# A routed expert layer whose row movements go per slot of an expert instead of per tile of tokens

## The reference

```python
logits = xf @ Wg                                  # 2048 x 8
probs = jax.nn.softmax(logits, axis=-1)
top_vals, top_idx = jax.lax.top_k(probs, 2)
onehot = one_hot(top_idx.T.reshape(-1), 8)        # 4096 choices, first choices first
loc = (cumsum(onehot, axis=0) - 1) at the chosen expert
keep = loc < 640
gates = top_vals * keep, divided by their sum
...
hid = inp @ W_in[e]                               # inp: the kept rows of expert e, 640 x 256; W_in[e]: 256 x 1024
a, g = jnp.split(hid, 2, axis=-1)
out_e = (gelu(a) * g) @ W_out[e]                  # W_out[e]: 512 x 256
y = sum over the 2 choices of gate * row loc of out_e   # x = x + y; xf is the layer-normed x
```

## Time and profile before

| | us |
|---|---|
| median of three runs (3078.27 to 3094.05) | 3084.43 |
| the profiled execution, own time | 3079.66 |
| its span in the profile | 3078.0 |
| layer L1f in the span (1736.9 to 2087.0) | 350.1 |

### The profile page before, as it was taken

The page is one execution under the profiler, slowest core; times in us unless marked ns, Lnnn a source line. Parts: engine busy times, 40 slices in busy tenths (PEclk is TensorE's granted clock), DMA queues, the critical chain, the costliest instruction groups (busy, mean ns, idle before and its releaser), DMA issues. The chain is left out here.

```text
span 3078.0 us, 84125 instructions
## 1 busy us (share of the span) xinstructions
PE 2585.4 (84%) x36049; PEld 2147.0 (70%) x36049; DVE 1781.5 (58%) x3347; ACT 1359.2 (44%) x3398; POOL 607.1 (20%) x740
## 2 busy tenths in 40 slices
PE   6999788999949999999987719937987766999888
PEld 5888556677737888888875519935774645888657
DVE  5777675566664444444455416636775766666563
ACT  3777323455523444444321204406773243666442
POOL 3111002121022111111102040042320533222200
PEclk9999899999979999999986659978998688999999
DMA  2110012111031000000000223322221001111100
GB/s 74 35 34 16 16 28 62 57 57 30 17 96 42 16 16 16 16 16 2 2 22 2 71 106 105 120 75 85 89 72 32 2 2 48 44 48 43 44 1 28
DMA packets 118717, 129.78 MB, mean 42 GB/s; under 512 B 10606, under 2 KB 109882, under 8 KB 118362
## 3 DMA queue, kind: packets, MB, share of 16 engines
q1 hardware_dynamic: 113882, 110.93, 11.7%
q0 software_dynamic: 4480, 13.64, 1.3%
HBM read 105.67 MB, written 18.88 MB: 40 GB/s over the span
## 5 line engine op out<-in xcount | busy, mean ns | idle before, releaser
L940 ACT ACTIVATE s_ca_probs<-s_ca_scores,s_ca_neg_max 128x256 f32<-128x256 f32 x768 | 353.3, 483 | 12.0 <-DVE s_ca_neg_max L983 8.8
L983 DVE TENSOR_REDUCE s_ca_neg_max<-s_ca_scores 128x4 f32<-128x1024 f32 x192 | 234.2, 1221 | 102.6 <-PE s_ca_scores L851 54.6
L863 PE MATMUL s_ca_probs_flipped<-identity,s_ca_probs 128*128 128x128 f32 x1536 | 212.6, 282 | 15.9 <-ACT s_ca_probs L940 9.8
L1314 DVE RECIPROCAL s_cc_inv_sums<-s_cc_sums 128x512 f32<-128x512 f32 x32 | 107.5, 3358 | 182.5 <-PE s_cc_out L1214 182.5
L863 PEld LDWEIGHTS s_ca_probs_flipped<-identity,s_ca_probs 128*128 128x128 f32 x1536 | 167.5, 143 | 58.6 <-ACT s_ca_probs L940 26.3
L1928 DVE COPY s_mx_w_mixed<-s_mx_ps 128x512 f32<-128x512 f32 x256 | 163.8, 684 | 60.3 <-PE s_mx_ps L1775 45.1
L946 ACT COPY s_ca_probsT<-s_ca_probs_flipped 128x512 f32<-128x512 f32 x192 | 114.7, 597 | 173.0 <-PE s_ca_probs_flipped L863 173.0
L1883 ACT COPY s_mx_w_mixed<-s_mx_ps 128x512 f32<-128x512 f32 x256 | 137.3, 589 | 115.3 <-PE s_mx_ps L1762 95.2
L550 PE MATMUL s_ln_flip<-identity,s_ln_xn 128*128 128x128 f32 x352 | 64.9, 368 | 139.5 <-DVE s_ln_xn L532 139.2
L1134 POOL TENSOR_TENSOR s_cc_probs_of_both<-s_cc_probsT 128x1024 f32<-128x1024 f32 x32 | 76.8, 2400 | 521.1 <-DVE s_cc_probsT L1305 521.1
L777 POOL TENSOR_TENSOR s_ca_inv_spread<-s_ca_inv_sums,h_ca_own_half 128x128 f32<-128x128 f32 x192 | 72.6, 399 | 472.8 <-DVE s_ca_inv_sums L1004 472.8
(11 more groups left out here) (462 smaller groups left out, 7250.8 us busy)
## 6 DMA issues: line engine op xcount, KB each, us to landing
h_ca_ctxT<-in_ctxT SPq DMA_DIRECT2D x96, 256.0 KB, 3.0
h_mx_w_by_input<-in_L_ffn_eW1T SPq DMA_DIRECT2D x16, 512.0 KB, 5.2
h_mx_w_by_hidden<-in_L_ffn_eW2T SPq DMA_DIRECT2D x8, 1024.0 KB, 6.3
s_re_win<-in_L_ffn_W_in SPq DMA_DIRECT2D x8, 1024.0 KB, 7.1
h_ca_ctx<-in_ctx SPq DMA_DIRECT2D x32, 256.0 KB, 2.8
x_normed_transposed<-in_ctx SPq DMA_DIRECT2D x7, 1024.0 KB, 5.5
expert_queues<-s_rt_zeros SPq DMA_DIRECT2D x5, 1024.0 KB
s_re_rows<-expert_queues SPq DMA_DIRECT2D x8, 640.0 KB, 5.1
```

The lines of the kernel that those rows point to most:

```text
L863: last = nc.tensor.transpose(psT[:, 2 * a + c, :], PR[b % 2][:, 4 * n + a, c * P:(c + 1) * P], ident[:, :])
L940: last = nc.scalar.activation(PR[b % 2][:, p, :], psS[:, p // 2, (p % 2) * NKEY:(p % 2 + 1) * NKEY], ACT.Exp, bias=nmax[b % 2][:, p:p + 1] ...
L983: nc.vector.tensor_reduce(nmax[b % 2][:, 4 * n:4 * n + 4], psS[:, 2 * n:2 * n + 2, :].rearrange("p r (g k) -> p r g k", g=GR), AX_X, ALU.m ...
L1314: nc.vector.reciprocal(RD[:, :, :], psD[:, :, :]).then_inc(s_rd, 1)
```

## The change

The row movements go by slot of an expert (8 x 640 slots in 40 tiles of 128) instead of by tile of choices.

- The small weights, the constants and expert 0's weights are loaded in the normalisation stage, and TensorE computes the logits there, two pairs of tiles behind its transposes.
- The new router stage `route_tokens` keeps softmax, choices and counts. SP stores the normalised rows as they are (`xrows`, 2 MB), zeroes `results` (4 MB, one row for each choice and a spare row for each slot) and loads expert 1's weights. Expert 0's weights are split by ACT and GpSimd. DVE compares each choice's place with a counting row, so that a sum of 32 multiplications on TensorE gives for each slot the number of the choice that lies in it. From it come `TOKN` (which token's row to gather) and `SLOT` (which row of `results` to write). GpSimd gathers the rows of experts 0 and 1 with 10 indirect DMAs at the end of this stage.
- In `routed_experts` GpSimd gathers the five row tiles of expert e + 2 and scatters the five result tiles of expert e, with 5 indirect DMAs each. The loop is written out. No instruction of TensorE's `up`, `down` or `flip` changes.
- The final stage is gone: at the end of `routed_experts` SP waits for the scatters and loads the results with 16 contiguous DMAs of 256 KB in eight groups into `XN` and `XNT`; DVE adds and takes statistics per group of two tiles, with the same 32 + 16 instructions.

```diff
+class ExpertWeights:
...
+        self.XR = [sb("re_rows", [P, QT, DIM]) for _ in range(2)]
+        self.WI, self.WO = sb("re_win", [P, KC, 2 * F]), sb("re_wout", [P, F // P, DIM])
...
+        self.xrows = nc.dram_tensor("expert_inputs", (TOKENS, DIM), F32, kind="Internal").ap()
+        self.results = nc.dram_tensor("choice_results", (2 * TILES * P + self.E * self.CAP, DIM), F32, kind="Internal").ap()
...
+    def load(self, sp):
+        d = self.d
+        sp.dma_start(self.WG[:, :, :], rows_to_sbuf(d["L1_ffn_Wg"])).then_inc(self.s_wg, 16)
...
+        self.load_in(sp, 0)
+        self.load_out(sp, 0)
+    def gather(self, pool, e):
+        QT = self.CAP // P
+        for n in range(e * QT, (e + 1) * QT):
+            pool.indirect_dma_start(self.XR[e % 2][:, n - e * QT, :], None, self.xrows,
+                                    bass.IndirectOffsetOnAxis(self.TOKN[:, n:n + 1], 0)).then_inc(self.s_r[e % 2], 16)
+    def logits(self, pe, XNT, u):
+        if u == 0:
+            pe.wait_ge(self.s_wg, 16)
+        for t in (2 * u, 2 * u + 1):
+            for c in range(KC):
+                pe.matmul(self.psL[:, t * self.E:(t + 1) * self.E], XNT[:, c, t * P:(t + 1) * P], self.WG[:, c, :],
+                          start=(c == 0), stop=(c == KC - 1))
...
+                    if logits and u >= 2:
+                        pe.wait_ge(s_out, u - 1)
+                        logits(pe, XNT, u - 2)
+                if logits:
+                    for u in range(NU - 2, NU):
+                        pe.wait_ge(s_out, u + 1)
+                        logits(pe, XNT, u)
...
+def route_tokens(nc, XN, ones, held):
...
+            @block.sync
+            def _(sp):
+                for h in range(2):
+                    t = slice(h * TILES // 2, (h + 1) * TILES // 2)
+                    sp.dma_start(xrows.rearrange("(t p) n -> p t n", p=P)[:, t, :], XN[:, t, :]).then_inc(s_x, 16)
+                sp.wait_ge(s_z, 1)
+                for r in range(0, CHOICES * P, ZR):
+                    sp.dma_start(results[r:r + ZR].rearrange("(a p) n -> p a n", p=P), Z[:, :, :]).then_inc(s_q, 16)
+                sp.wait_ge(s_il, KC)
+                held.load_in(sp, 1)
+                sp.wait_ge(s_ol, 1)
+                held.load_out(sp, 1)
+                sp.wait_ge(s_q, 16 * (CHOICES * P // ZR))
+            @block.gpsimd
+            def _(pool):
+                nc.gpsimd.memset(Z[:, :, :], 0.0).then_inc(s_z, 1)
+                for c in range(KC):
+                    pool.wait_ge(s_ih, c + 1)
+                    nc.gpsimd.tensor_tensor(WIS[0][1][:, c, :], WI[:, c, :], WIS[0][0][:, c, :].bitcast(F32), ALU.subtract).then_inc(s_il, 1)
+                pool.wait_ge(s_oh, 1)
+                nc.gpsimd.tensor_tensor(WOS[0][1][:, :, :], WO[:, :, :], WOS[0][0][:, :, :].bitcast(F32), ALU.subtract).then_inc(s_ol, 1)
+                pool.wait_ge(s_eq, 1)
+                nc.gpsimd.tensor_tensor(B[:, :, 1, :], EQ[:, :, :], NUM[:, :].unsqueeze(2).broadcast_to([P, CHOICES, SLOTS]),
+                                        ALU.mult).then_inc(s_b, 1)
+                pool.wait_ge(s_x, 32)
+                pool.wait_ge(s_tok, 1)
+                held.gather(pool, 0)
+                held.gather(pool, 1)
+            @block.tensor
+            def _(pe):
+                pe.wait_ge(s_c0, 64)
+                nc.tensor.matmul(psN[:, 0:P], ones[:, :], BE[:, :], start=True, stop=True).then_inc(s_io, 1)
+                pe.wait_ge(s_ohc, 1)
+                flat = OH[:, :, :, :].rearrange("p k t e -> p (k t e)")
+                nc.tensor.matmul(psR[:, 0:CHOICES * E], BE[:, :], flat, start=True, stop=True)
+                nc.tensor.matmul(psT[:, 0:CHOICES * E], ones[:, :], flat, start=True, stop=True).then_inc(s_cn, 1)
+                pe.wait_ge(s_b, 2)
+                for n in range(CHOICES):
+                    pe.wait_ge(s_a, n // GROUP + 1)
+                    last = nc.tensor.matmul(psI[:, 0:2 * SLOTS], A[:, n, :], B[:, n, :, :].rearrange("p a h -> p (a h)"),
+                                            start=(n == 0), stop=(n == CHOICES - 1))
+                last.then_inc(s_in, 1)
...
+                act.wait_ge(s_io, 1)
+                nc.scalar.copy(IOTA[:, :], psN[:, 0:P]).then_inc(s_ct, 1)
+                act.wait_ge(s_mx, 1)
+                nc.scalar.activation(PRB[:, :, :], L[:, :, :], ACT.Exp).then_inc(s_e, 1)
+                for c in range(KC):
+                    act.wait_ge(held.s_wi, 16)
+                    nc.scalar.copy(WIS[0][0][:, c, :], WI[:, c, :]).then_inc(s_ih, 1)
+                act.wait_ge(held.s_wo, 16)
+                nc.scalar.copy(WOS[0][0][:, :, :], WO[:, :, :]).then_inc(s_oh, 1)
...
+                nc.vector.tensor_reduce(kept[:, :], KM[:, :, :], AX_X, ALU.add)
+                nc.vector.tensor_tensor(KB[:, :, :], KM[:, :, :], BASE[:, :].unsqueeze(1).broadcast_to(C), ALU.mult)
+                link(nc.vector.tensor_tensor(PLACE[:, :, :], PLACE[:, :, :], KM[:, :, :], ALU.mult))
+                nc.vector.tensor_scalar(far[:, :], kept[:, :], -1000.0, 1000.0, ALU.mult, ALU.add)
+                nc.vector.tensor_reduce(start[:, :], KB[:, :, :], AX_X, ALU.add)
+                link(nc.vector.tensor_reduce(loc[:, :], PLACE[:, :, :], AX_X, ALU.add))
+                nc.vector.scalar_tensor_tensor(far[:, :], start[:, :], 1.0 / P, far[:, :], ALU.mult, ALU.add)
+                link(nc.vector.tensor_scalar(q[:, :], loc[:, :], float(P), None, ALU.is_ge))
+                for j in range(2, QT):
+                    link(nc.vector.scalar_tensor_tensor(q[:, :], loc[:, :], float(j * P), q[:, :], ALU.is_ge, ALU.add))
+                nc.vector.scalar_tensor_tensor(lo[:, :], q[:, :], -float(P), loc[:, :], ALU.mult, ALU.add)
+                link(nc.vector.tensor_tensor(hi[:, :], q[:, :], far[:, :], ALU.add))
+                dve.wait_ge(s_ct, 1)
+                nc.vector.tensor_tensor(EQ[:, :, :], hi[:, :].unsqueeze(2).broadcast_to([P, CHOICES, SLOTS]),
+                                        IOTA[:, 0:SLOTS].unsqueeze(1).broadcast_to([P, CHOICES, SLOTS]), ALU.is_equal).then_inc(s_eq, 1)
+                dve.wait_ge(s_eq, 1)
+                nc.vector.tensor_scalar(B[:, :, 0, :], EQ[:, :, :], LANE[:, 0:1], None, ALU.mult).then_inc(s_b, 1)
+                for g in range(CHOICES // GROUP):
+                    n = slice(g * GROUP, (g + 1) * GROUP)
+                    nc.vector.tensor_tensor(A[:, n, :], lo[:, n].unsqueeze(2).broadcast_to([P, GROUP, P]),
+                                            IOTA[:, :].unsqueeze(1).broadcast_to([P, GROUP, P]), ALU.is_equal).then_inc(s_a, 1)
+                nc.vector.tensor_scalar(dump[:, :], IOTA[:, 0:SLOTS], float(P), LANE[:, 0:1], ALU.mult, ALU.add)
+                dve.wait_ge(s_in, 1)
+                link(nc.vector.tensor_copy(tile_of[:, :], psI[:, SLOTS:2 * SLOTS]))
+                link(nc.vector.scalar_tensor_tensor(number[:, :], tile_of[:, :], float(P), psI[:, 0:SLOTS], ALU.mult, ALU.add))
...
+                nc.vector.tensor_copy(TOKN[:, :], token[:, :]).then_inc(s_tok, 1)
...
+                nc.vector.tensor_copy(SLOT[:, :], number[:, :])
...
+def routed_experts(nc, X, ST, XNT, XN, ident, held):
...
+        YG = [XN[:, :, :], XNT[:, :, :].rearrange("p c n -> p (c n)").rearrange("p (t n) -> p t n", n=DIM)]
...
+            @block.sync
+            def _(sp):
+                for e in range(2, E):
+                    sp.wait_ge(s_il, e * KC)
+                    held.load_in(sp, e)
+                    sp.wait_ge(s_ol, e)
+                    held.load_out(sp, e)
+                for u in range(2):
+                    sp.wait_ge(s_st[u], 16 * QT * (E // 2))
+                for g in range(GROUPS):
+                    for k in range(2):
+                        r = (k * TILES + g * TG) * P
+                        sp.dma_start(YG[k][:, g * TG:(g + 1) * TG, :], results[r:r + TG * P].rearrange("(t p) n -> p t n", p=P)).then_inc(s_g[g], 16)
+            @block.gpsimd
+            def _(pool):
+                for e in range(E):
+                    if e + 2 < E:
+                        pool.wait_ge(s_fl, (e + 1) * QT)
+                        held.gather(pool, e + 2)
+                    for j in range(QT):
+                        n = e * QT + j
+                        pool.wait_ge(s_yr, n + 1)
+                        nc.gpsimd.indirect_dma_start(results, bass.IndirectOffsetOnAxis(SLOT[:, n:n + 1], 0),
+                                                     YR[e % 2][:, j, :], None).then_inc(s_st[e % 2], 16)
...
         if "L1f" in STAGES:
-            with nc.sbuf_tensor("x_normed", [P, TILES, DIM], F32) as XN:
-                layernorm_transposed(nc, X, XNT, ident, ST, rows=XN)
-                routed_experts(nc, X, ST, XNT, XN, ident, ones, d)
+            with nc.sbuf_tensor("x_normed", [P, TILES, DIM], F32) as XN, held(nc, kept) as (sb, sem):
+                w = ExpertWeights(nc, sb, sem, d)
+                with nc.psum_tensor("rt_psl", [P, 512], F32) as w.psL:
```

(9 more changed lines are left out.)

636 lines of the change are left out of this document (280 added, 356 removed).

## The result

The changed kernel takes 3023.99 us (median of 4 runs, 3015.32 to 3030.09) against 3082.8 for the kernel before beside it: a ratio of 0.9819, 95% interval 0.98 to 0.9838. It is faster by 58.8 us; the forecast was 3034. Its profiled execution took 3015.32 us, span 3013.5.

The account below looks back on a forecast made before the run. GpSimd alone was taken to bound two stretches (43.1 and 54.4 us), TensorE the 192.2 us between. Terms -21.1 and -28.0 sum to -49.1, giving 3035.3 against the runs' median, stated as 3034; range 3023 to 3046, outer limits 3012 and 3054.

Parts of the forecast that it names:

- Both main terms: Layer's head up to the first projection, -21.1 us, and tail from last result store to next stage, -28.0 us.
- I take the half clock for the mixture: Normalisation: transposes and logits together take 20.25 us with logits at half clock; router's first DVE instruction -4.5 us.
- The rival at 0.14: Normalisation: the clock rises beside the logits, -7.3 us, 3027 us in all; chance 0.14.
- Router chain: Router from its first DVE instruction to the first gather: 31.3 us, plus 8.2 for the lock.
- R: Router's first DVE instruction, forecast to move from 1765.07 to 1760.6.
- the lock: Router: GpSimd's subtractions block DVE's two-input chain, about 6 us, and `B`'s half blocks `A`, +2.2; +8.2 together.
- Seam: Stage change behind the ten gathers: 1.5 us, between 0.7 and 3.5.
- So 0: Experts' steady part: last gather lands 4.0 us early in a 22.7 us period, so gathers and scatters cost 0.
- the 2.0 us for the receipt: Tail: 2.0 us added behind the last scatter's landing until the semaphore is seen, between 0 and 2.8.
- Contiguous loads: Tail: first two loads take 3.0 and 0.4 us; 4.2 MB at 349 GB/s, 12 us, so DVE's 18.3 bounds.
- The sum: Whole kernel: -21.1 - 28.0 = -49.1 us, forecast 3034 us; chance 0.58.
- the likeliest case's own range: Range of the sum, the case given 0.58: 3023 to 3046 us.

Follow-up runs that it names:

- first profile: Profiled execution of the changed kernel from its first measurement, against the kernel before: 3015.32 us, layer 290.95 us; median of that comparison 3023.99 us.
- chip A: Set of four edited versions of the changed kernel (logits back, splits on DVE, five or ten gathers behind the seam), no unaltered one: 3018.42, 3016.54, 3012.88, 3020.33 us.
- chips B and C: Two further sets of four runs, each with the changed kernel unaltered beside edited versions and the kernel before; unaltered: 3035.25 us on B, 3031.29 on C.

## Why the prediction was right

- *Both main terms* were right in kind: -21.1 us to the first projection, measured -27.0 (102.96 to 75.93 from the layer's start), and -28.0 from there to the end, measured -31.5 (246.5 to 215.0). GpSimd's two stretches went, and nothing took their place in the first profile.
- *Logits:* the step that failed is "I take the half clock for the mixture". The rival at 0.14, -7.3, came true with -6.5, in seven of twelve profiles. In the other five the router started 22.8 us behind the layer against 23.1 said: there the step holds. The profile of before had its clock at full shortly ahead of the layer, as these five have; the argument from the share of the logits could not tell the two groups apart.
- *Router chain:* 38.2 against 39.5. The exponential came 2.7 us behind R (2.8 said), the sums took 7.02 (6.9 said, by the logits' pitch of 0.216 for few columns), the lock held DVE three times, for some 5.6 in total (6 said), and for 2.2 at `B`, where DVE's half took 3.06 instead of the 0.89 that it takes alone (2.2 said, but for the wrong instruction: the prediction had `A` held, and it was `B`'s first half, which reads one tile of SBUF). For two inputs the Trainium skill ("SBUF — State Buffer", Who interferes with whom) says that such a DVE instruction and a GpSimd one that reads SBUF exclude each other for the whole instruction; moving the splits to DVE brought the first gather 5.6 us forward, which bears it out.
- *Seam:* 1.5 taken, 3.8 measured, above the upper bound of 3.5. The step counted it from the end of the last issue and left out that the gather has still to land: 2.7 us from its start and 0.8 of bare seam make 2.6 of the 3.8. The remaining 1.2 may be of the kind that stood behind the scatters before, 3.5 beyond landing; no run parts it.
- *Steady part:* "So 0" was right in the first profile and on chip A (188.4 to 189.5 us in those five profiles, from first projection to last copy) and wrong on chips B and C by 6 to 8 us. The rows were never late, as argued; a gather costs there through small instructions of ScalarE and DVE, not through its pitch. I had priced this cover by one resource, GpSimd's time. That the stretch came 2.1 us short in the first profile was not forecast either: 1.3 from first projection to last result copy (190.13 to 188.86), which I took as unchanged, and 0.9 because the last scatter started 0.7 us behind that copy and not 1.6.
- *Tail:* the 2.0 us for the receipt were not there. Landing and receipt together took 2.50 us from the start of the last issue. The Trainium skill ("DMA: Bandwidth & Descriptors", Anatomy of one DMA) puts a fixed cost of about 2 us mostly to the write receipt; by this row it lies within the landing time that the profile gives, and isn't added to it. Contiguous loads held: the first two were there 3.4 us after the first issue, as said, and after that DVE's pace bound (18.7 us, 18.3 said). Gathers in their place cost 27.6 more.
- *The sum:* the layer is 9.4 us shorter than said in the first profile, and 1.7 and 3.4 shorter on chips B and C, where the clock's gain and the holes nearly cancel; that is luck, since neither is in the sum. 3023.99 lies at the low end of the likeliest case's own range. In its three comparisons the unaltered kernel is 58.8, 42.9 and 43.6 us below the kernel before (ratios 0.9819, 0.984 and 0.9846), with layers 58.5, 50.8 and 52.5 us shorter than that of the one profile of before. On chips B and C the median shows 8 to 9 us less than the layer. The kernel before was itself 4.6 and 7.9 us faster there than in the first comparison; which part of it was is not known, since it has one profile.

What stays open: what a GELU with its product ready waits for, and why chip A shows no holes. Fetching instructions is not it: the instruction queues moved 16 packets in the first profile's stretch and 16 in that of chip B, and in the 11 us ahead of the hole shown above (1933 to 1944) not one, so none came late there either. A queue of GpSimd's that is spread over fewer DMA engines was not tried.

## What to carry over

Price a transfer that is laid beside the bound engine not only by whether its data come in time, but by what it does to the small instructions in the bound engine's loop; measure this on more than one chip before trusting 0. Put indirect DMAs whose data the next stage needs late behind the stage's end, and leave those that it needs at once in front of it: five moved brought the first projection 6.2 us forward, all ten 4.5, although only then the seam was short. And keep two-input work of GpSimd away from a linked chain on VectorE, even when GpSimd is otherwise idle: the same three subtractions cost 5.6 us of path on GpSimd and none on VectorE inside its wait.

## What the runs showed of the hardware

- A stage's end costs 0.8 us behind DVE's last instruction where no indirect DMA is near. It came 3.8 to 3.9 us behind the last of five or ten gathers, and in one kernel with 32 gathers 5.1 us behind DVE's last instruction, 9.2 behind the last gather; in the kernel before, with 32 gathers too, 0.7 and 7.1.
- The granted clock beside the same transposes and logits was 1.00 for most of them in seven profiles, where it had been at 0.50 shortly before the layer, and 0.50 throughout in five, where it had been at 1.00: 16.6 or 22.8 us. That the one causes the other is not shown.
- Indirect gathers beside GELUs: 6 to 8 us of holes on two chips, none on another; without the gathers 0.9 of 6.2 are left, without the scatters 2.6; with the gathers doubled TensorE was idle for 28 us, at a clock of 0.92 instead of 0.98.
- A GpSimd gather's issue, 0.95 us, was stretched to 1.83 beside a two-input DVE instruction of 1.23 us; in that profile TensorE never waited for a gather.
